# A fourth score bank, biases that wait by twos, an earlier read of the moved q and k, and x loaded in pieces

## The reference

```python
q = rmsnorm(xn @ Wq.T) ; k = rmsnorm(xn @ Wk.T) ; v = xn @ Wv.T     # 32 query heads, 8 key/value heads, 128 wide
scores = q @ k.T / sqrt(128)
bias = where(rel > 0, -1e30, slope[head] * rel)                      # causal, rel = key position - query position
s = (softmax(scores + bias) @ v) @ Wo.T                              # four query heads share one key/value head
f = 2 * einsum(low, B, 8 * softmax(xn @ Wr.T + br))                  # low = xn @ A.T, eight experts of rank 16
y = x + s * silu(f)
```

## Time and profile before

| | us |
|---|---|
| median of 3 runs (lowest, highest) | 812.68 (811.22, 815.48) |
| the profiled execution | 817.76 |
| its span | 815.9 |

### The profile page before, as it was taken

How to read it: one execution, slowest core, us unless ns; L and a number is a source line. 1 busy time by engine, 2 the same in 40 slices (tenths; PEclk the granted TensorE clock), 3 DMA queues, 4 the chain that set the end, 5 groups by cost and what they waited for, 6 DMA issues and landing times.

```text
span 815.9 us, 14699 instructions
## 1 busy us (share of the span) xinstructions
PE 741.8 (91%) x3729; PEld 618.2 (76%) x3729; DVE 583.6 (72%) x1378; ACT 560.9 (69%) x1370; POOL 397.6 (49%) x423
## 2 busy tenths in 40 slices
PE   8888989989999799979999799997999799998877
PEld 7777867868787687868788687876887687787666
DVE  7855687676876688666886669776886668777465
ACT  4655767677676677667676766766777666778773
POOL 5313454446444563554544564445525536446447
PEclk9999999999999899989999899998999999999989
DMA  7015848577585757776485675857577674856832
GB/s 277 2 35 135 260 123 242 150 210 208 150 264 143 222 157 223 199 212 204 129 256 161 179 206 146 265 140 220 160 211 207 191 231 115 235 166 185 259 98 91
DMA packets 214707, 148.27 MB, mean 182 GB/s; under 512 B 48896, under 2 KB 205440, under 8 KB 214528
## 3 DMA queue, kind: packets, MB, share of 16 engines
q1 hardware_dynamic: 214656, 147.77, 62.7%
HBM read 85.84 MB, written 61.87 MB: 181 GB/s over the span
## 4 chain that ended last, share of the span: by engine, by line
PE 29%; issue 28%; POOL 21%; DVE 7%; ACT 5%; DMA 4%; SPq 3%; DVEq 0%; POOLq 0%; ACTq 0%
POOL pt_lo L515 9%; POOL inv_rms L505 6%; PE qkv_ps L1136 4%; PE qkv_ps L1137 3%; PE qkv_ps L1138 3%; POOL w_lo L486 3%; DMA qk_moved<-turning_qk 3%; SPq L419 3%; PE out_ps L1136 3%; PE score_ps L1136 3%; PE out_ps L1137 2%; PE out_ps L1138 2%; PE score_ps L1138 2%; PE score_ps L1137 2%; DVE sums L932 2%
## 5 line engine op out<-in xcount | busy, mean ns | idle before, releaser
L515 POOL TENSOR_TENSOR pt_lo<-x_sb,pt_hi 128x512 fp32r<-128x512 f32 x153 | 194.4, 1297 | 242.5 <-ACT pt_hi L677 242.5
L1136 PE MATMUL qkv_ps<-w_hi,xt_hi 128*128 128x512 f32 (+1 forms) x512 | 176.9, 346 | 16.7 <-DVE qk_norm L948 9.1
L884 DVE CUSTOM_DVE_ANT_0 probs<-score_ps,cst,slope 128x128 f32<-128x128 f32 (+3 forms) x256 | 130.6, 545 | 85.3 <-PE score_ps L1138 52.6
L625 ACT ACTIVATE probs<-probs,neg_max 128x128 f32<-128x128 f32 (+3 forms) x256 | 141.7, 556 | 54.2 <-DVE neg_max L884 53.3
L1137 PE MATMUL qkv_ps<-w_lo,xt_hi 128*128 128x512 f32 (+1 forms) x512 | 173.9, 340 | 0.0
L1138 PE MATMUL qkv_ps<-w_hi,xt_lo 128*128 128x512 f32 (+1 forms) x512 | 172.8, 337 | 0.0
L633 ACT ACTIVATE probs<-probs,recip 128x128 f32<-128x128 f32 (+3 forms) x252 | 122.5, 549 | 12.2 <-DVE recip L891 12.2
L1136 PEld LDWEIGHTS qkv_ps<-w_hi,xt_hi 128*128 128x128 f32 x512 | 96.9, 189 | 40.9 <-DVE qk_norm L948 13.8
L903 DVE STREAM_TRANSPOSE squared<-probs 128x256 f32<-128x256 f32 (+3 forms) x124 | 99.0, 821 | 23.5 <-ACT probs L633 20.2
L1136 PE MATMUL score_ps<-k_hi,q_hi 128*128 128x256 f32 (+2 forms) x192 | 72.2, 376 | 38.0 <-DVE neg_max L884 29.6
L1136 PE MATMUL out_ps<-wo_hi,o_hi 128*128 128x512 f32 x252 | 104.8, 416 | 2.0 <-DVE o_lo L926 2.0
(11 more groups left out here) (157 smaller groups left out, 1432.3 us busy)
## 6 DMA issues: line engine op xcount, KB each, us to landing
turning_qk<-squares SPq DMA_DIRECT2D x240, 80.0 KB, 1.9
qk_moved<-turning_qk SPq DMA_DIRECT2D x60, 320.0 KB, 3.2
turning<-squared SPq DMA_DIRECT2D x120, 128.0 KB, 2.2
x_sb<-turning SPq DMA_DIRECT2D x30, 512.0 KB, 5.1
w_raw<-wqkv SPq DMA_DIRECT2D x32, 384.0 KB, 5.4
turning<-squared SPq DMA_DIRECT2D x120, 96.0 KB, 1.9
x_sb<-turning SPq DMA_DIRECT2D x30, 384.0 KB, 4.1
turning<-squared SPq DMA_DIRECT2D x128, 64.0 KB, 1.7
```

The costliest lines, as they stand in the source:

```text
L515: nc.gpsimd.tensor_tensor(by_quad(pt_lo, j), moved_block(t, j), by_quad(pt_hi, j).bitcast(F32), ALU.subtract).then_inc(pt_lo_by_pool, 1)
L625: nc.scalar.activation(probs[:, h, 0:n], probs[:, h, 0:n], ACT.Exp, bias=neg_max[:, h:h + 1], scale=-1.0, accum_out=total[:, h:h + 1]).the ...
L884: nc.vector.tensor_tensor_reduce(probs[:, h, 0:n], score_bank(t, h), cst[:, C_DIST + SEQ - n:C_DIST + SEQ], slope[:, h:h + 1], HUGE, ALU.a ...
L1136: pe.matmul(out, a_hi, b_hi, start=start, stop=False)
```

## The change

- `score_bank` gives head 3 a bank of its own (`turn_ps`, which nothing else uses after slot 2 until `end`) in slots above 2, and `scores` then doesn't wait for head 0's bias. In `end` the last unit keeps three banks.
- `bias` waits once for two heads (and adds once to the unused count `scores_taken`): for heads 2 and 3 in all slots above 2, for heads 0 and 1 too where there are one or two blocks of keys.
- `move` puts the read of the moved q and k between the writes of the two halves of the probabilities.
- ACT's slot 5 copies the third and the fourth chunk of the weights together, ahead of q_hi.
- x is loaded the second time in eight DMAs of 256 KB: two at the end of SP's last slots 3 and 4, four at the end of the last slot 5. POOL waits for all of them.

```diff
+            n = keys_of(t) * P
+            if h == 3 and has_own_bank(t, at_end):
+                return turn_ps[:, 0:n]
+            return score_ps[:, h % (3 if t >= 2 else 2), 0:n]
+
+        def has_own_bank(t, at_end=False):
+            return t > 2 and not at_end
...
-                if u is not None:
-                    sp.wait_ge(qk_written, QK_WRITTEN(g, u - BY_TURN, 16 * QUADS))
-                    sp.dma_start(qk_moved[:, :, :], ...).then_inc(qk_moved_ready, 16)
+                    if u is not None and pair == 0:
+                        sp.wait_ge(qk_written, QK_WRITTEN(g, u - BY_TURN, 16 * QUADS))
+                        sp.dma_start(qk_moved[:, :, :], ...).then_inc(qk_moved_ready, 16)
...
-                if left == 1 and t == 3:
+                if left == 1:
+                    load_x_again(range(2 * (t - 3), 2 * (t - 3) + 2))
+                if left == 1 and t == BY_PE - 1:
+                    load_x_again(range(BLOCKS - 2, BLOCKS))
...
+                for m in blocks:
+                    sp.dma_start(x_late[m], x[m * P:(m + 1) * P, :]).then_inc(x_again, 16)
...
                 if w_due:
-                    split_w(g + 1, range(2, 3))
+                    split_w(g + 1, range(EARLY_W, KC))
...
-                if w_due:
-                    split_w(g + 1, range(3, KC))
...
-                dve.wait_ge(scores_ready, PER_HEAD(g, t, h + 1))
-                if t > 0 and h % 2 == 0 and not at_end:
-                    dve.wait_ge(probs_squared, TWO(g, t - 1, h // 2 + 1))
-                dve.sem_inc(scores_taken, 1)
+                by_twos = t > 2 and not at_end and (h >= 2 or keys_of(t) <= 2)
+                if not (by_twos and h % 2 == 1):
+                    dve.wait_ge(scores_ready, PER_HEAD(g, t, h + (2 if by_twos else 1)))
+                    if t > 0 and h % 2 == 0 and not at_end:
+                        dve.wait_ge(probs_squared, TWO(g, t - 1, h // 2 + 1))
+                    dve.sem_inc(scores_taken, 1)
...
-                elif h == 3:
+                elif h == 3 and not has_own_bank(t, at_end):
                     pe.wait_ge(biased_ready, PER_HEAD(g, t, 1))
```

More of the change, by code:

```diff
@@ L350, in turned_qk, with score_bank @@
             return turned_ps(u) if u < BY_TURN else (qk_moved_by_head[:, 0:HPG, :, :], qk_moved_by_head[:, HPG, :, :])
-        def score_bank(t, h):
-            return score_ps[:, h % (3 if t >= 2 else 2), 0:keys_of(t) * P]
+        def score_bank(t, h, at_end=False):
+            n = keys_of(t) * P
[4 more added lines that the diff above has]
+            return t > 2 and not at_end
         def last_turns(t):
@@ L446, in slot, with load_x_again @@
                     next_wo(g, t - 6)
-                if left == 1 and t == 3:
+                if left == 1:
+                    load_x_again(range(2 * (t - 3), 2 * (t - 3) + 2))
+                if left == 1 and t == BY_PE - 1:
+                    load_x_again(range(BLOCKS - 2, BLOCKS))
+            def load_x_again(blocks):
+                if 0 in blocks:
                     sp.wait_ge(qkv_ready, ONE(GROUPS - 1, 0, 1))
-                    sp.dma_start(w_raw[:, :, :].rearrange("p c n -> p (c n)").rearrange("p (t n) -> p t n", n=DM),
-                                 x[0:(BLOCKS - 2) * P, :].rearrange("(t p) n -> p t n", p=P)).then_inc(x_again, 16)
+                if BLOCKS - 1 in blocks:
                     sp.wait_ge(wo_lo_done, GROUPS * HPG)
-                    sp.dma_start(wo_raw[:, 0:2, :], x[(BLOCKS - 2) * P:BLOCKS * P, :].rearrange("(t p) n -> p t n", p=P)).then_inc(x_again, 16)
+                for m in blocks:
+                    sp.dma_start(x_late[m], x[m * P:(m + 1) * P, :]).then_inc(x_again, 16)
             sp.wait_ge(xt_turned, BLOCKS)
@@ L544, in end @@
                 pool.wait_ge(gate_done, 1)
-                pool.wait_ge(x_again, 32)
+                pool.wait_ge(x_again, 16 * BLOCKS)
                 for m in range(3):
@@ L1220, in gate_in, with scores @@
                       True, True).then_inc(gate_in_done, 1)
-            def scores(g, t, h):
+            def scores(g, t, h, at_end=False):
                 n, hs, b = keys_of(t) * P, slice(h * HD, (h + 1) * HD), t // QB % BATCH
@@ L1237, in scores @@
                     pe.wait_ge(biased_ready, PER_HEAD(g, t, 0))
-                elif h == 3:
+                elif h == 3 and not has_own_bank(t, at_end):
                     pe.wait_ge(biased_ready, PER_HEAD(g, t, 1))
-                out = score_bank(t, h)
+                out = score_bank(t, h, at_end)
                 if t % QB == 0:
@@ L1331, in end @@
                 for h in range(3):
-                    scores(g, last, h)
+                    scores(g, last, h, at_end=True)
                 mix(g, before - 1, 1)
@@ L1335, in end @@
                     turn_probs(before, n)
-                scores(g, last, 3)
+                scores(g, last, 3, at_end=True)
                 out(g, before - 1)
```

4 lines of the change are left out of this document (2 added, 2 removed).

## The result

| | us, median (lowest, highest) | ratio to before, 95% interval |
|---|---|---|
| before | 814.08 (811.22, 818.15), 4 runs | |
| after | 826.52 (824.46, 827.89), 4 runs | 1.0147 (1.0094 to 1.0200) |
| profiled execution, before | 817.76, span 815.9 | |
| profiled execution, after | 825.6, span 823.7 | |

The changed kernel is 12.4 us slower where 21 us less were forecast, outside the range of 777 to 809.

What follows compares the result with a forecast made beforehand. PE, 91% busy, was taken as the bound, its project waiting on the qk_norm chain. Terms 10.4 - 5.4 + 5.9 + 8.4 + 2.1 = 21.4 us off 812.68 gave 791 us, own range 784 to 800, overall range 777 to 809.

Steps and rivals of the forecast that it cites:

- Term 1: Slot 3 to slot 5 at the loop's jumps: own bank and earlier read gain 1.7 us in six rounds, 10.4 us.
- The read is in the way: Rival: the read's 320 KB delay the second half's writes 1.1 us, 14 times; 15 us less gain, 806 us; chance 0.18.
- Slower: Rival: SP stands until q and k are written, delaying the second half; 2.5 us in 14 places, 826 us; chance 0.07.
- Edits at nothing: Waits for two heads at once; saved waits and increments put between 0 and 0.7 us, taken as 0.
- Term 2: PE's granted clock falls after new idles before slot 5's project: 0.9 us in each of six rounds, 5.4 us lost.
- Term 3: w_hi copied together in slot 5: PE's project no longer waits for POOL's w_lo, 5.9 us gained over seven places.
- Term 4: Slots 7 to 9: earlier bias and ACT's shorter waits for q and k gain 1.2 us seven times, 8.4 us.
- Term 5: Last group: x loaded in pieces no longer delays writes, and PE's wait before head 3 goes; 2.1 us gained.

Runs made afterwards that it cites:

- e1: The changed kernel with the read of the moved q and k put back behind both halves' writes: 796.4 us, ratio 0.9758 to the kernel before.
- e2: The kernel before with the moved read alone, between the two halves' writes: 826.4 us, ratio 1.0107.
- e5: The changed kernel with only a quarter of the read (80 of 320 KB) between the halves' writes, the rest behind both: 807.9 us, ratio 0.9926 to before.
- e16: e1 with the read split in two transfers (80 and 240 KB), both behind the two halves' writes: 811.8 us, ratio 0.9980 to before.
- e4: The kernel before with the fourth bank alone, so head 3's scores don't wait for a bias: 809.6 us, ratio 0.9941.
- e3: The kernel before with the biases' waits by twos alone: 798.8 us, ratio 0.9790.
- e7: e1 with the last chunk of w_hi split apart from the others again, behind the probabilities: 800.4 us, ratio 0.9829 to before.
- e11: The kernel before with w_hi split in one stretch alone: 811.4 us, ratio 0.9984.
- e8: e1 with x loaded again in two transfers, not eight pieces: 796.4 us, ratio 0.9785 to before.
- e17: e1 with the read split in three transfers (16, 64 and 240 KB), all behind both halves' writes: 831.5 us, ratio 1.0215 to before.
- e12: The changed kernel with the whole read behind both halves' writes and behind the first read of the probabilities: 828.1 us, ratio 1.0186 to before.

## Why the prediction was wrong

- **The step that failed** is in Term 1, the new place of the read. The forecast took it as a gain of 1.8 us at the jump and priced it at "one issue of 0.45 us between the halves of the writes", with nothing for the writes behind it. The runs show a loss in its place: 30 us with the other edits (e1) and 11 us alone (e2), with the second half's 128 KB writes landing in 3.0 us instead of 2.2.
- **The read is in the way** was the rival with this mechanism, and should have been the forecast. Its delay a place was right: it said 1.1 us, and SP's waits for the second half are 70 us longer than in e1, in 62 places. Its count was not. It took 14 places, the two stretches of each round, and 15 us. The read changed its place in all 60 moves, and 30 us are 0.5 us a move. Against e1 the profiled execution lost 27.8 us: 15.3 in the seven stretches from slot 3 to 5, 4.7 in the seven from slot 7 to 9, and 7.8 outside of both. On the kernel before (e2) the 14 stretches are even 2.2 us shorter together while the span is 9.3 us longer, so there the loss is wholly where I hadn't looked. That "before the change the same bytes were ahead of the reads" overlooked that the reads also wait for the second half's writes to land, and these now come behind. The Trainium skill (DMA: Bandwidth & Descriptors, "HWDGE ordering") states that each DMA engine takes descriptors in ring order; the later landing of the writes behind the read agrees with it.
- **Slower** gave the right time, for the wrong reason: its stand of SP is real (46.6 us), but e5 against e16 shows no price for a stand of 33.4. That SP was "nowhere seen to stand long" for these writes was not quite so: the kernel before has two such waits, one of 2.8 us.
- **Term 1.** With the read put back the stretch is even shorter than forecast: the six stretches from slot 3 to slot 5 are 31.8 to 33.4 us, mean 32.8, where I said 34.1; before they were 35.8. The windows of e1 for the fourth of them (columns as in rows 8):

```profile
442.71:475.21 32.50, 28.24 (x145) 23.51 (x144) 23.54 (x56) 25.82 (x64) 21.60 (x22) 1.00 0.78 226
475.21:481.05 5.84, 5.84 (x24) 5.05 (x25) 5.84 (x9) 2.49 (x6) 3.94 (x3) 0.71 0.23 56
```

  That is 18 us of the 19 by which e1's six rounds are shorter. But the cause isn't the one of the term. I gave it to the bank and to the earlier read. With the bank alone (e4) the mean is 34.5, with the read alone (e2) 35.1, and with the waits by twos alone (e3) 32.4 (read from their PE timelines in the same way): most is DVE's 3.03 us, which I read as "the jump itself" and carried along as fixed. In the changed kernel the mean is 34.8, near the forecast of 34.1, by two errors that nearly cancel: the stand that went and the read that costs 2.0 us here.
- **Edits at nothing.** "What a wait and an increment less save" was bounded by 0.7 us; it was 16 us alone, the largest term of all. The bound was taken from a row that has nothing to do with it; the 42 packets of the instruction queue were on the page, and I made nothing of them.
- **Term 2.** PE does wait 2 to 3 us for qk_norm in slot 5, and the granted clock does fall behind it: 0.71 over the 5.84 us above, after 2.64 us of standing; in the changed kernel it is 0.71 too, after 2.95 us. But in the whole stretch before it the clock is 1.00 in both, where the jump alone had 6.7 us at 0.50. In the changed kernel the two nearly cancel (a mean clock of 0.969 for 0.971), and without the read between the gain is larger (0.981 in e1, 0.994 in e3). So the loss of 5.4 us is not seen. (3 us at 0.54 are also 1.4 us lost, not 1.5.)
- **Term 3** (5.9 us): the wait for w_lo is gone as said; it is worth 4 to 6 us with the other edits (e7), and alone (e11) nothing that can be told, 5.9 us being outside its interval. What keeps the time up there is open: PE's waits for qk_norm and for the biases are 7.3 and 30.4 us (9.1 and 29.6 before).
- **Term 4** (8.4 us): not seen. The stretch from slot 7 to slot 9 has a mean of 29.9 us over e1's seven (28.9 to 31.1), 30.2 before and 30.6 in the changed kernel. That is nearest to the term's lower bound of 0.
- **Term 5** (2.1 us): nothing (e8).

What stays open: where exactly the step in the number of instructions lies, by what the second transfer costs 15 us (e16) when most of its issuing is hidden, and how the 20 us between two and three transfers (e16, e17) divide between issue and small packets.

## What to carry to other kernels

A queue that one engine fills in order is a chain of its own: price a DMA moved or added in it in every slot in which it is issued, not only where the matmul engine waits today, and ask what lands behind it. Idle time at a loop's jump with "issue" behind it isn't fixed: compare the instruction queue's packets, and try a few waits fewer on that engine before anything larger. A large wait in the profile of an engine that isn't the bottleneck (61 us of ACT for q and k) need not be worth shortening, and is no slack either: pushed 58 us further, it cost 32 (e12).

## What I had not expected of the hardware

- DVE stood 3 us at each of six jumps with 14699 and 14615 instructions executed by all engines (42 packets, 0.34 MB of instruction loads), and not with 14525, the difference being DVE's alone (11 packets, 0.09 MB).
- One more DMA of 0.45 us of issuing a move, with the same bytes, cost 15 us over the kernel.
- With a read of 320 KB put ahead of the second half's four writes, the writes of 128 KB land in 3.0 us in the median instead of 2.2, and with the same read on another engine's queue in 2.8.
